# Edge counts by a fixed table, early one-hots, weight sums in K/V, and two jobs back on VectorE, in a fused graph and attention kernel

## The chip, the cores and the metric

The kernel runs on one core of a Trainium2 chip, as one program with one launch. TensorE multiplies matrices into eight PSUM banks; VectorE, ScalarE and GpSimd work on elements; SyncE's queue issues all the DMAs. The metric is the device time of one execution in microseconds (us). Before the change it is 1457.32 us, the median of 3 runs (1456.39 to 1459.52).

## What is computed

The input is `x`, 1250 nodes by 1024 features, a list of 20,000 edges (`src`, `dst`), and weights. One layer is computed:

```
xn = layernorm(x)
x  = x + gnn(xn) + mix(xn)
x  = x + ffn(layernorm(x))

mix: q = relu(xn Wq + bq); k = relu(xn Wk + bk); v = xn Wv + bv
     attn = q (k^T v) / (L * 64), 16 heads; attn Wo + bo
gnn: sage(h, Ws, Wn, b) = h Ws + (A h / deg) Wn + b
     h = relu(sage(xn, Ws0, Wn0, b0)); sage(h, Ws1, Wn1, b1)
ffn: both weights are rounded to -1, 0, 1 times mean(|w|), activations to 127 steps per row
     gelu(xq w1) w2
```

`A` is the matrix of edge counts, 1250 by 1250: entry (d, s) is how many edges go from s to d. The edges are sorted by `dst`.

## The kernel before

Rows of x are worked through in ten tiles of 128. Matrices that need more than half precision are held as a high and a low half in 16 bits, and a product of two such is three passes of matmuls: `product` (line 1384) runs over eight steps kc of 128 rows, each six matmuls of 128x512, 48 in all. The high half is a ScalarE copy, the low half is the value minus the high half, on VectorE.

The stages in order, with TensorE's line for each:

- *K/V*: for each tile k, then v; `kv_sum` (line 1435) adds the tile's k^T v into PSUM. TensorE's order for a tile t is k of t, `kv_sum` of t - 1, the transposes of x for t + 1, v of t. `kv_sum` of t needs the low half of v of t. Beside it, ScalarE adds up squares and absolute values of the weights in chunks of 128x1024 that pass through a ring of four slots, `STREAM`: each tile from 1 to 8 takes six chunks for norms and two for means (line 588), 64 in all, and all of them stand on ScalarE ahead of the high half of v (`v_hi`, line 535). A chunk's load is issued by SyncE when the sum four chunks before it has ended. In tiles 4 to 7 ScalarE also takes the high halves of two chunks of Wq there.
- *Q and M*: q for eight column tiles m (line 1502), and M = (k^T v) Wo for the heads (line 1510). ScalarE takes six chunks of absolute values with each m (line 610), 48 in all.
- *U*: U = q M for ten tiles (line 1398), with `x` and the biases added on the way out: GpSimd adds the biases to x (line 450), VectorE adds that to the product (line 1122), and the sum goes to a scratch in DRAM. U is in units of four banks, and beside it the edge counts are made.
- *z0*: xn Wn0 for ten tiles, with the rest of the counts. After it come the sums over edges, h, z1, and the feed-forward part, which the change does not touch.

The *edge counts* come from one-hots. VectorE compares a constant ramp with each edge's key (`count_dve`, lines 1110 and 1112), two one-hots per chunk of 128 edges, four chunks to a group, in a ring of four groups that lies in `STREAM`. TensorE multiplies the two (`count_pe`, line 1568), four matmuls a group, into one of four banks. The edges fall into 40 ranges of `dst`, and so into parts 1 to 40, with a part 0 that takes the first chunks of the first range. ScalarE copies each finished range out (line 655). Before the change, tile 0 of U has part 0 ahead of its last step, every later tile of U and z0 has two parts, ahead of steps 3 and 6, and the last tile of z0 has parts 37 to 40. The first one-hots can be made only when all 112 weight sums have ended (`stream_used`), because they overwrite `STREAM`; VectorE makes them after the last low half of M.

The weights Wn0 (in U) and Ws0 (in z0) are also split: SyncE loads a chunk into `SPLIT`, ScalarE makes the high half and a scaled copy (lines 516 and 503), and GpSimd subtracts (line 454). Ws0 lies where M was, so its loads are issued after U.

Every engine runs its own program in the order in which it is written; semaphores join them. No planner decides anything.

## Time and profile before

| what | value |
|---|---|
| runs | 1456.39, 1457.32, 1459.52 us |
| profiled execution | 1456.9 us, span 1454.8 us |
| TensorE busy | 1397.5 us, 96% of the span |
| VectorE, ScalarE, GpSimd busy | 738.8, 483.8, 72.9 us |
| chain that ended last | TensorE 70%, VectorE 14%, issue 5%, DMA 5%, ScalarE 4% |
| mean granted clock of TensorE | 0.991 |

The span is the time between the first and the last instruction of the core. Busy time is summed per engine. In the rows below PE is TensorE, PEld its weight loads, DVE VectorE, ACT ScalarE, POOL GpSimd and SPq SyncE's queue; L588 is line 588 of the kernel before. A bracket at a row's end is the time that the engine was idle before it, and the work whose end released it. The granted clock is a share of full speed.

### The profile page before, as it was taken

Reading aid. Unit: us, or ns where it says so; the run is one execution under the profiler, and the core shown is the slowest. Engines: PE = TensorE matmul, PEld = TensorE weight load, DVE = VectorE, ACT = ScalarE, POOL = GpSimd, SP = SyncE. Lnnn points to the kernel's source line nnn. Section 1 sums busy time; section 2 is a strip of 40 time slices with the busy share of each in tenths; the row PEclk is TensorE's granted clock in tenths of the full one; section 3 lists DMA queues with packets and bytes.
Section 4 is the critical chain, followed back from the end, with each engine's and each line's share of the span. In section 5 each row is a group of like instructions: output and inputs, shape, how many; then the busy total and the mean of one; then the engine's idle time right before and its main releaser. Section 6 shows DMA issues by size and latency. Waiting matters only on the chain.

```text
span 1454.8 us, 22724 instructions
## 1 busy us (share of the span) xinstructions
PE 1397.5 (96%) x7442; PEld 677.5 (47%) x7443; DVE 738.8 (51%) x1292; ACT 483.8 (33%) x664; POOL 72.9 (5%) x55
## 2 busy tenths in 40 slices
PE   4999999999699999999999999999999999999998
PEld 2454445555245444444444444444444444444444
DVE  6735452353598645527667422147888453333332
ACT  7646574266412123211221222100000244443342
POOL 0000000000223311100000000000000000000000
PEclk9999999999899999999999999999999999999999
DMA  8356762786323231024455112154564211000100
GB/s 318 104 215 215 263 222 111 261 285 217 143 88 131 101 102 45 15 73 129 146 159 161 41 46 71 72 205 131 185 202 144 100 74 59 30 29 29 58 29 29
DMA packets 55523, 183.13 MB, mean 126 GB/s; under 512 B 6176, under 2 KB 14880, under 8 KB 55200
## 3 DMA queue, kind: packets, MB, share of 16 engines
q1 hardware_dynamic: 55456, 182.26, 36.4%
q8 instruction: 40, 0.66, 0.2%
q14 instruction: 27, 0.22, 0.1%
HBM read 158.11 MB, written 24.12 MB: 125 GB/s over the span
## 4 chain that ended last, share of the span: by engine, by line
PE 70%; DVE 14%; issue 5%; DMA 5%; ACT 4%; DVEq 1%; SPq 1%; ACTq 0%
PE ps L1398 34%; PE ps L1749 10%; PE ps L1735 9%; PE ps L1502 7%; PE ps L1634 4%; DMA SPLIT<-in_Wneigh 3%; DVE XIN L1204 2%; PE ps L1568 2%; DVE SPLIT L1204 2%; PE ps L1405 2%; DVE XIN L1198 1%; DVE SPLIT L1198 1%; DMA STREAM<-in_w1t 1%; PE ps L1435 1%; ACT S L503 1%
## 5 line engine op out<-in xcount | busy, mean ns | idle before, releaser
L1398 PE MATMUL ps<-S,XH 128*128 128x512 f16 x2400 | 529.4, 380 | 1.3 <-ACT XH L710 0.8
L1398 PEld LDWEIGHTS ps<-S,XH 128*128 (+1 forms) x2400 | 232.3, 98 | 274.0 <-issue 1.1
L1634 PE MATMUL ps<-Zb,AT 128*128 128x512 f16 x800 | 177.3, 382 | 7.4 <-DVE TMP L1220 7.4
L1749 PE MATMUL ps<-S,XH 128*128 128x512 fp8e4 x640 | 143.0, 379 | 1.1 <-ACT XH L776 1.1
L1735 PE MATMUL ps<-S,SPLIT 128*128 128x512 fp8e4 x640 | 141.2, 379 | 0.0
L1634 PEld LDWEIGHTS ps<-Zb,AT 128*128 (+1 forms) x800 | 78.0, 98 | 104.7 <-issue 13.0
L1110 DVE TENSOR_SCALAR STREAM<-iota_m,key_m 128x320 f16 x240 | 107.4, 447 | 24.6 <-issue 18.1
L1398 PE MATMUL ps<-Zb,XH 128*128 128x512 f16 x480 | 107.7, 384 | 4.6 <-ACT Zb L503 2.3
L1398 PE MATMUL ps<-S,Zb 128*128 128x512 f16 x480 | 107.3, 380 | 0.0
L1502 PE MATMUL ps<-XH,S 128*128 128x512 f16 (+1 forms) x576 | 102.6, 339 | 0.0
L1735 PEld LDWEIGHTS ps<-S,SPLIT 128*128 128x128 f16 x640 | 62.2, 98 | 73.2
L1749 PEld LDWEIGHTS ps<-S,XH 128*128 128x128 f16 x640 | 61.3, 98 | 69.8 <-issue 1.4
L764 ACT ACTIVATE Zb<-ps,cols 128x512 f32<-128x512 f32 x80 | 54.5, 686 | 118.1 <-PE ps L1735 118.0
L1324 DVE TENSOR_REDUCE AM<-Zb 128x1 f32<-128x1024 f32 x40 | 48.2, 1216 | 58.8 <-ACT Zb L764 58.8
L1502 PEld LDWEIGHTS ps<-XH,S 128*128 128x128 f16 x576 | 56.1, 98 | 47.0 <-issue 2.3
L1398 PEld LDWEIGHTS ps<-Zb,XH 128*128 128x128 f16 x480 | 47.3, 99 | 62.0 <-issue 4.4
L588 ACT ACTIVATE STREAM<-STREAM 128x1024 f32<-128x1024 f32 x64 | 66.9, 1045 | 17.9 <-DMA STREAM<-in_w1t 15.7
L655 ACT ACTIVATE AT<-ps 128x320 f32 (+1 forms) x40 | 17.4, 436 | 165.6 <-PE ps L1573 165.6
L1398 PEld LDWEIGHTS ps<-S,Zb 128*128 (+1 forms) x480 | 45.7, 98 | 53.6 <-issue 1.1
L1112 DVE TENSOR_SCALAR STREAM<-iota_s,key_s 128x128 f16 x240 | 65.4, 273 | 0.0
L1568 PE MATMUL ps<-STREAM 128*128 x240 | 43.3, 310 | 16.8 <-DVE STREAM L1112 16.6
L610 ACT ACTIVATE STREAM<-STREAM 128x1024 f32<-128x1024 f32 x48 | 50.3, 1050 | 17.0 <-DMA STREAM<-in_w2t 11.0
(202 smaller groups left out, 1168.1 us busy)
## 6 DMA issues: line engine op xcount, KB each, us to landing
STREAM<-in_w1t SPq DMA_DIRECT2D x64, 512.0 KB, 4.7
STREAM<-in_w2t SPq DMA_DIRECT2D x64, 512.0 KB, 4.7
STREAM<-in_w_all SPq DMA_DIRECT2D x48, 512.0 KB, 5.7
XIN<-in_x SPq DMA_DIRECT2D x20, 512.0 KB, 5.3
SPLIT<-in_Wneigh SPq DMA_DIRECT2D x16, 512.0 KB, 5.7
SPLIT<-in_Wself SPq DMA_DIRECT2D x16, 512.0 KB, 3.5
u_scratch<-HL SPq DMA_DIRECT2D x10, 512.0 KB, 3.0
XIN<-u_scratch SPq DMA_DIRECT2D x10, 512.0 KB, 6.2
```

The costliest lines, as they stand in the source:

```text
L588: A(STREAM[:, n % 4, :], STREAM[:, n % 4, :], ACT.Square if n < NORMS else ACT.Abs, accum_out=total).then_inc(S("stream_used"), 1)
L610: A(STREAM[:, slot, :], STREAM[:, slot, :], ACT.Abs, accum_out=MW_all[:, bass.ds(c, 1)]).then_inc(S("stream_used"), 1)
L764: A(hid[:, slot, n * BANK:(n + 1) * BANK], banks(n % 4, 1), ACT.Gelu, scale=at("dq1", t)).then_inc(S("gelu"), 1)
L1110: V.tensor_scalar(hot_m[:, bass.ds(r * QUAD + j, 1), :], iota_m[:, :], key_m[:, bass.ds(c_ + j, 1)], None, ALU.is_equal)
L1112: one = V.tensor_scalar(hot_s[:, bass.ds(r * QUAD + j, 1), :], iota_s[:, :], key_s[:, bass.ds(c_ + j, 1)], -float(g * P), ALU.subtract, AL ...
L1204: V.scalar_tensor_tensor(q8[:, n % 2, :], STREAM[:, n, :], col("nthr")[:, w:w + 1], above, ALU.is_lt, ALU.subtract, saturate=False).then_i ...
L1398: last = mm(acc[:, n * BANK:(n + 1) * BANK], left(l, kc), right(kc, r)[:, n * BANK:(n + 1) * BANK], start=(kc == 0 and i == 0), stop=(kc = ...
L1502: last = mm(ps[:, 3 * j * BANK + a:3 * j * BANK + b], Wq_s[:, kc, l, mc], XH[:, r, kc, a:b], start=(kc == 0 and l == 0 and r == 0), stop=( ...
L1568: one = mm(ps[:, at_:at_ + GW], hot_s[:, bass.ds(r * QUAD + q, 1), :], hot_m[:, bass.ds(r * QUAD + q, 1), :], start=False, stop=False, ski ...
L1634: last = mm(banks(bank + n, 1), AT_tile(t, s), Z[:, r, s, n * BANK:(n + 1) * BANK], start=(s == 0 and r == 0), stop=(s == NT - 1 and r == 1))
L1735: last = mm(banks(n % 4, 1), x2_tile[:, j, kc, :], w1q[:, kc, n * BANK:(n + 1) * BANK], start=(kc == 0), stop=(kc == KC - 1))
L1749: last = mm(banks(4 + h, 1), hid_T[:, j, kc, :], w2q[:, kc, h * BANK:(h + 1) * BANK], start=(kc == 0), stop=(kc == HC - 1))
```

## The change

- *Sums.* In K/V each tile takes four chunks of absolute values instead of two, four more come after tile 8, and Q takes four with each of m = 0 to 6, none with m = 7. It remains 112 in all.
- *Early one-hots.* VectorE makes part 0, now three groups instead of four, between q's tiles 6 and 7.
- *Counts by table.* `PARTS` gives the number of parts for each tile of U and z0: one in the first four, two in the next ten, three in the next five, two in the last. One part stands ahead of step 6 (7 in the first tile), two ahead of 3 and 6, three ahead of 2, 4 and 6.
- *VectorE.* GpSimd's additions and subtractions go. VectorE subtracts from the scaled chunk in one operation, and adds the biases to the result of U in a second operation behind the first. In a tile it makes the one-hots of the first part, then the work of the tile before (the result of U or the low half of z0, then the split), then the other one-hots. In U, chunk t of Wn0 is split in tile t + 2; in z0, chunk t of Ws0 in tile t.
- *x and Wn0* are loaded two chunks ahead; the loads of x for U come ahead of the weight chunks of Q.
- The loops over U and z0 are written out.

```diff
-NORMS, KV_MEANS = 6, 2
-Q_MEANS = 6
-Q_FIRST = 8 * KV_MEANS
+NORMS, KV_MEANS = 6, 4
+KV_ALL = NORMS + KV_MEANS
+Q_MEANS = 4
+Q_FIRST = 8 * KV_MEANS + 4
 RING = 4
-FIRST_PART = RING * QUAD
+FIRST_PART = 3 * QUAD
 NB = NG + 1
 LO_UNIT = 256
+PARTS = [1] * 4 + [2] * 10 + [3] * 5 + [2]
+        def parts_of(tile):
+            return range(sum(PARTS[:tile]), sum(PARTS[:tile + 1]))
-                for n in range(NORMS + KV_MEANS):
-                    slot = n % 4
+                for n in range(KV_ALL):
+                    slot = (2 * j + n) % 4
                     if first and n < 4:
                         sp.wait_ge(S("split_lo"), KC + n + 1)
-                    wait(sp, "stream_used", (NORMS + KV_MEANS) * (t - 1) + n - 3)
+                    wait(sp, "stream_used", KV_ALL * (t - 1) + n - 3)
                     chunk = rows(w_all, NORMS * (t - 1) + n) if n < NORMS else \
                         rows(w_flat[0], KV_MEANS * (t - 1) + n - NORMS)
                     sp.dma_start(STREAM[:, slot, :], chunk).then_inc(S(f"stream_in{slot}"), 16)
...
+            def mean_load(w, c, slot):
+                sp.wait_ge(S("stream_used"), c + (8 * NORMS - 3))
+                sp.dma_start(STREAM[:, slot, :], rows(w_flat[w], c - HC * w)).then_inc(S(f"stream_in{slot}"), 16)
+            for n in range(4):
+                mean_load(1, 8 * KV_MEANS + n, n)
...
-            mean_loads(0, Q_FIRST, HC)
-            mean_loads(1, HC, 2 * HC)
             sp.wait_ge(S("ln_xn"), NT)
             load_x(0, 0)
             load_x(1, 1)
-            load_split(Wneigh0, 0, 0, 24)
+            mean_loads(1, Q_FIRST, 2 * HC)
+            for t in range(2):
+                load_split(Wneigh0, t, t, 24 + t)
             def u_moves(t, j, split=True, x_too=True):
                 if split:
-                    load_split(Wneigh0, t + 1, 1 - j, 24 + 1 + t)
+                    load_split(Wneigh0, t, j, 24 + t)
...
-            steps(sp, 0, 6, u_moves)
-            u_moves(6, 0)
-            u_moves(7, 1, False)
+            steps(sp, 0, 2, lambda t, j: u_moves(t, j, split=False))
+            steps(sp, 2, 8, u_moves)
...
-            def u_pool(t, j):
-                pool.wait_ge(S(f"x_in{j}"), 80 + 8 * (t - j) + 16)
-                nc.gpsimd.tensor_tensor(XIN[:, j, :], XIN[:, j, :], b_out, ALU.add).then_inc(S("xb"), 1)
-            def split_pool(dst, kc, slot, idx):
-                pool.wait_ge(S("split_hi"), idx + 1)
-                nc.gpsimd.tensor_tensor(dst[:, kc, 1, :], SPLIT[:, slot, :], dst[:, kc, 0, :],
-                                        ALU.subtract).then_inc(S("split_lo"), 1)
-            def u_split_pool(t, j):
-                u_pool(t, j)
-                split_pool(weight(S0), t, j, 24 + t)
-            pool.wait_ge(S("b_out"), 1)
-            pool.wait_ge(S("split_lo"), 24)
-            steps(pool, 0, 8, u_split_pool)
-            for t in range(8, NT):
-                u_pool(t, t % 2)
-            steps(pool, 0, 8, lambda t, j: split_pool(weight(S1), t, j, 32 + t))
...
-            def split_scaled(dst, kc, slot, idx, scale):
-                act.wait_ge(S(f"split_in{slot}"), 8 * (idx - KC * WQ - slot) + 16)
-                alone(act)
-                A(dst[:, kc, 0, :], SPLIT[:, slot, :], ACT.Copy, scale=scale)
-                split(SPLIT[:, slot, :], SPLIT[:, slot, :], scale)
...
-                    for n in range(NORMS + KV_MEANS):
+                    for n in range(KV_ALL):
...
-                        act.wait_ge(S(f"stream_in{n % 4}"), 32 * (t - 1) + 16 * (n // 4) + 16)
+                        b = 1 - j
+                        slot = (2 * b + n) % 4
+                        act.wait_ge(S(f"stream_in{slot}"), 40 * (t - (1 + b)) + 16 * ((10 * b + n) // 4) + 16)
                         alone(act)
...
+            norm("norm5", 5, 4)
+            for n in range(4):
+                add_up(8 * KV_MEANS + n, n, 20 * 16 + 16)
+            kv_act(9, 1, ln=False, norms=False)
...
+            def q_means(m):
                 for n in range(Q_MEANS):
-                    at_ = Q_MEANS * j + n
-                    add_up(Q_FIRST + Q_MEANS * m + n, at_ % 4, 16 * 16 + 24 * (m - j) + 16 * (at_ // 4) + 16)
+                    add_up(Q_FIRST + Q_MEANS * m + n, n, 21 * 16 + 16 * m + 16)
...
-            q_means(7, 1)
...
+            def counts_act(tile):
+                for part in parts_of(tile):
...
+            for t in range(NT):
+                if t > 1:
+                    split_chunk(weight(S0), t - 2, t % 2, 24 + t - 2, at("s", WN0))
+                counts_act(t)
...
+            for t in range(NT):
+                if t > 0:
+                    z_act("z0", t - 1, 4 * ((t - 1) % 2), Z0_SCALE)
+                if t < KC:
+                    split_chunk(weight(S1), t, t % 2, 32 + t, at("s", WS0))
+                counts_act(NT + t)
...
-            steps(dve, 4, 8, qm_dve)
-            for p in range(5, KC):
-                m_dve(p, M_BANK[p])
-            dve.wait_ge(S("b_out_in"), 32)
-            V.tensor_tensor(b_out, b1_in, b_out, ALU.add).then_inc(S("b_out"), 1)
...
-            def u_out_dve(t, j, first=False):
-                dve.wait_ge(S("u_ps"), t + 1)
-                dve.wait_ge(S("xb"), t + 1)
...
+            steps(dve, 4, 6, qm_dve)
+            qm_dve(6, 0)
             dve.wait_ge(S("bounds"), 1)
             dve.wait_ge(S("iotas"), 3)
             dve.wait_ge(S("stream_used"), 112)
             count_dve(0)
+            qm_dve(7, 1)
+            for p in range(5, KC):
+                m_dve(p, M_BANK[p])
+            dve.wait_ge(S("b_out_in"), 32)
+            V.tensor_tensor(b_out, b1_in, b_out, ALU.add).then_inc(S("b_out"), 1)
+            def u_out_dve(t, j, first=False):
+                dve.wait_ge(S("u_ps"), t + 1)
+                dve.wait_ge(S(f"x_in{j}"), 80 + 8 * (t - j) + 16)
+                if not first:
+                    dve.wait_ge(S(f"u_out{j}"), 8 * (t - j))
+                V.scalar_tensor_tensor(u_out[:, j, :], banks(4 * j), c, XIN[:, j, :],
+                                       ALU.mult, ALU.add).then_inc(S("u_t"), 1)
+                dve.wait_ge(S("u_t"), t + 1)
+                V.tensor_tensor(u_out[:, j, :], u_out[:, j, :], b_out, ALU.add).then_inc(S("u"), 1)
+            def counts_dve(tile, between):
+                parts = list(parts_of(tile))
+                count_dve(parts[0])
+                between()
+                for part in parts[1:]:
+                    count_dve(part)
...
+            def u_dve(t):
+                u_out_dve(t - 1, (t - 1) % 2, t < 3)
+                if t > 1:
+                    split_chunk(weight(S0), t - 2, t % 2, 24 + t - 2, at("s", WN0))
+            dve.wait_ge(S("b_out"), 1)
             for t in range(1, NT):
-                u_dve(t)
+                counts_dve(t, lambda: u_dve(t))
...
             def z0_dve(t):
-                count_dve(2 * t + 19)
                 if t > 0:
                     z_dve("z0", t - 1, 4 * ((t - 1) % 2), Z0_SCALE)
                 else:
                     u_out_dve(9, 1)
-                count_dve(2 * t + 20)
-            z0_dve(0)
-            z0_dve(1)
+                if t < KC:
+                    split_chunk(weight(S1), t, t % 2, 32 + t, at("s", WS0))
+            for t in range(2):
+                counts_dve(NT + t, lambda: z0_dve(t))
...
-            for t in range(2, 9):
-                z0_dve(t)
-            count_dve(37)
-            z_dve("z0", 8, 0, Z0_SCALE)
-            for part in range(38, NB):
-                count_dve(part)
+            for t in range(2, NT):
+                counts_dve(NT + t, lambda: z0_dve(t))
             z_dve("z0", 9, 4, Z0_SCALE)
-            dve.wait_ge(S("split_lo"), 40)
...
-            def counts_between(first_part, j):
-                return {3: lambda: count_pe(first_part, count_bank(2 - 2 * j)),
-                        6: lambda: count_pe(first_part + 1, count_bank(3 - 2 * j))}
-            def u_pe(pair, j, ready=None, between=None):
-                t = pair * 2 + j
+            def counts_between(tile, more={}):
+                parts = list(parts_of(tile))
+                places = {1: (7 if tile == 0 else 6,), 2: (3, 6), 3: (2, 4, 6)}[len(parts)]
...
+            def u_pe(t):
                 wait(pe, "u", t - 1)
-                product(banks(4 * j), lambda l, p: qT[:, l, p, tile_of(t)], of(M_s), ready, "m",
-                        between or counts_between(t * 2 - 1, j)).then_inc(S("u_ps"), 1)
+                product(banks(4 * (t % 2)), lambda l, p: qT[:, l, p, tile_of(t)], of(M_s), 0 if t == 0 else None, "m",
+                        counts_between(t, {7: lambda: pe.wait_ge(S("m_lo"), 8)} if t == 0 else {}))\
+                    .then_inc(S("u_ps"), 1)
...
+            for t in range(NT):
+                u_pe(t)
...
+            def z0_pe(t, more={}):
+                wait(pe, "z0_lo", t - 1)
+                product(banks(4 * (t % 2)), of_x(t), of(weight(S0)),
+                        between=counts_between(NT + t, more)).then_inc(S("z0_ps"), 1)
...
-            z0_pe(4, 1, {3: lambda: count_pe(37, count_bank(0)), 5: lambda: count_pe(38, count_bank(1)),
-                         6: lambda: count_pe(39, count_bank(2)), 7: lambda: count_pe(40, count_bank(3))})
+            for t in range(2, NT):
+                z0_pe(t)
```

On ScalarE, at the last K/V tiles: the sums (written to `NPW` or `MW`) stand ahead of the second copy to `AT`, the high half of v. Before:

```order
L495 ACTIVATE XH<-ps 128x8x128
L531 ACTIVATE AT<-TMP 128x1024
L588 ACTIVATE STREAM,NPW<-STREAM 128x1024 x6
L588 ACTIVATE STREAM,MW<-STREAM 128x1024 x2
L535 ACTIVATE AT<-TMP 128x1024
L500 ACTIVATE cols<-ps 128x5
L531 ACTIVATE AT<-TMP 128x1024
L535 ACTIVATE AT<-TMP 128x1024
```

and now:

```order
L481 ACTIVATE XH<-ps 128x8x128
L510 ACTIVATE AT<-TMP 128x1024
L569 ACTIVATE STREAM,NPW<-STREAM 128x1024 x6
L569 ACTIVATE STREAM,MW<-STREAM 128x1024 x4
L514 ACTIVATE AT<-TMP 128x1024
L486 ACTIVATE cols<-ps 128x5
L582 ACTIVATE STREAM,MW<-STREAM 128x1024 x4
L510 ACTIVATE AT<-TMP 128x1024
L514 ACTIVATE AT<-TMP 128x1024
```

Two more sums stand ahead of the high half, and four between the norms' square root and the high half of k of tile 9.

On VectorE, at the end of Q: `Zb<-AT,Zb` is q's low half, `S<-ps,cols,S` M's low half, and the load of `bnd` begins a part of one-hots. Before:

```order
L1072 SCALAR_TENSOR_TENSOR S<-ps,cols,S 128x1024
L221 REGISTER_ALU
L221 COMPARE_AND_BRANCH
L1072 SCALAR_TENSOR_TENSOR S<-ps,cols,S 128x1024 [waits m_hi] x3
L1087 TENSOR_TENSOR TMP<-AT,TMP 128x1024 [waits b_out_in]
L1100 TENSOR_LOAD bnd [waits stream_used,iotas,bounds]
```

and now:

```order
L954 TENSOR_SCALAR AT<-ps,cols 128x1250 [waits q_lo,q_ps]
L957 SCALAR_TENSOR_TENSOR Zb<-AT,Zb 128x1250 [waits q_hi]
L1034 SCALAR_TENSOR_TENSOR S<-ps,cols,S 128x1024 [waits m_hi]
L1054 TENSOR_LOAD bnd [waits stream_used,iotas,bounds]
...
L1066 TENSOR_SCALAR STREAM<-iota_s,key_s 128x128
L1069 ISA
L1057 COMPARE_AND_BRANCH
L954 TENSOR_SCALAR AT<-ps,cols 128x1250 [waits q_lo,q_ps]
L957 SCALAR_TENSOR_TENSOR Zb<-AT,Zb 128x1250 [waits q_hi]
L1034 SCALAR_TENSOR_TENSOR S<-ps,cols,S 128x1024 [waits m_hi] x4
L1081 TENSOR_TENSOR TMP<-AT,TMP 128x1024 [waits b_out_in]
```

The part that waits for `stream_used` has moved ahead of q's last tile, M's low halves and the addition of the biases.

On VectorE, in the first tile of z0: the result of U's last tile and what follows it. Before:

```order
L1112 TENSOR_SCALAR STREAM<-iota_s,key_s 128x128
L1115 ISA
L1103 COMPARE_AND_BRANCH
L1122 SCALAR_TENSOR_TENSOR HL<-ps,cols,XIN 128x1024 [waits u_out1,xb,u_ps]
L1100 TENSOR_LOAD bnd
```

and now:

```order
L1066 TENSOR_SCALAR STREAM<-iota_s,key_s 128x128
L1069 ISA
L1057 COMPARE_AND_BRANCH
L1088 SCALAR_TENSOR_TENSOR HL<-ps,cols,XIN 128x1024 [waits u_out1,x_in1,u_ps]
L1091 TENSOR_TENSOR HL<-HL,TMP 128x1024 [waits u_t]
L825 SCALAR_TENSOR_TENSOR S<-SPLIT,cols,S 128x1024 [waits split_hi]
L1054 TENSOR_LOAD bnd
```

Between U's last result and the next one-hots there are now the addition of the biases and the split of the first chunk of Ws0, which waits for ScalarE's high half.

## Rows read from the trace of the kernel before

**Rows 1.** Busy time by stretch: engines' us, granted clock, DMA share and rate.

```profile
60.00:257.00 197.00, 194.40 (x1145) 98.00 (x1145) 85.38 (x108) 112.50 (x178) 0.00 (x0) 1.00 0.56 198
384.80:404.20 19.40, 5.14 (x19) 1.83 (x18) 16.32 (x42) 4.79 (x6) 8.79 (x4) 0.58 0.19 75
434.10:446.74 12.64, 12.64 (x69) 6.35 (x68) 10.60 (x34) 2.88 (x5) 4.51 (x2) 1.00 0.37 126
634.00:637.00 3.00, 3.00 (x11) 1.19 (x11) 1.95 (x10) 0.44 (x1) 0.00 (x0) 0.50 0.00 0
```

**Rows 2.** Timeline of ScalarE, tile 4: start, us, line, idle before in brackets.

```profile
143.28 1.04 ACT L588 ACTIVATE STREAM<-STREAM 128x1024 f32<-128x1024 f32 x1
...
148.64 1.06 ACT L588 ACTIVATE STREAM<-STREAM 128x1024 f32<-128x1024 f32 x1 [2.61 <-DMA STREAM<-in_w1t]
...
149.70 1.04 ACT L535 ACTIVATE AT<-TMP 128x1024 f16<-128x1024 f32 x1
```

**Rows 3.** DMA issues, 142.3 to 144.8 us: count, KB, us to landing.

```profile
STREAM<-in_w1t SPq DMA_DIRECT2D x1, 512.0 KB, 5.9
XIN<-in_x SPq DMA_DIRECT2D x1, 512.0 KB, 6.6
SPLIT<-in_Wq SPq DMA_DIRECT2D x2, 512.0 KB, 7.6
```

**Rows 4.** Timeline of SyncE's queue, the same place.

```profile
142.52 0.33 SPq L277 DMA_DIRECT2D STREAM<-in_w1t  x1
143.05 0.33 SPq L239 DMA_DIRECT2D XIN<-in_x  x1
```

**Rows 5.** Timeline of TensorE: K-times-V sums of tiles 1, 4, 7.

```profile
81.97 1.50 PE L1435 MATMUL ps<-AT 128*128 128x128 f16 x24
...
152.14 1.50 PE L1435 MATMUL ps<-AT 128*128 128x128 f16 x24 [1.01 <-DVE AT L907]
...
222.91 1.50 PE L1435 MATMUL ps<-AT 128*128 128x128 f16 x24
```

**Rows 6.** Timeline of ScalarE: V high halves of tiles 1, 7.

```profile
78.17 1.04 ACT L535 ACTIVATE AT<-TMP 128x1024 f16<-128x1024 f32 x1
...
219.89 1.04 ACT L535 ACTIVATE AT<-TMP 128x1024 f16<-128x1024 f32 x1
```

**Rows 7.** Timeline of TensorE: the first edge counts.

```profile
388.84 1.28 PE L1568 MATMUL ps<-STREAM 128*128 x4 [4.02 <-DVE STREAM L1112]
...
401.23 1.26 PE L1568 MATMUL ps<-STREAM 128*128 x4 [8.91 <-DVE STREAM L1112]
```

**Rows 8.** Timelines of GpSimd and VectorE in TensorE's long wait.

```profile
391.90 2.33 POOL L450 TENSOR_TENSOR XIN<-XIN,TMP 128x1024 f32<-128x1024 f32 x1 [91.40 <-ACT SPLIT L503]
...
391.88 2.41 DVE L1112 TENSOR_SCALAR STREAM<-iota_s,key_s 128x128 f16 x1
```

**Rows 9.** Timeline of TensorE, last tile of z0.

```profile
633.28 1.22 PE L1568 MATMUL ps<-STREAM 128*128 x4 [2.37 <-DVE STREAM L1112]
```

**Rows 10.** Timelines of ScalarE and TensorE, first tile of z0.

```profile
528.47 1.15 ACT L516 ACTIVATE S<-SPLIT,cols 128x1024 f16<-128x1024 f32 x1 [10.71 <-DMA SPLIT<-in_Wself]
...
528.01 0.70 PE L1568 MATMUL ps<-STREAM 128*128 x4
```

**Rows 11.** Timelines of ScalarE and VectorE: weight sums, one-hots.

```profile
360.58 1.04 ACT L610 ACTIVATE STREAM<-STREAM 128x1024 f32<-128x1024 f32 x1
...
385.14 0.19 ACT L610 ACTIVATION_READ_ACCUMULATOR STREAM<-STREAM 128x1 f32 x1
...
367.94 1.58 DVE L992 TENSOR_SCALAR AT<-ps,cols 128x1250 f32<-128x1250 f32 x1 [8.47 <-PE ps L1502]
...
378.23 1.22 DVE L1087 TENSOR_TENSOR TMP<-AT,TMP 128x1024 f32<-128x1024 f32 x1
...
386.86 0.30 DVE L1110 TENSOR_SCALAR STREAM<-iota_m,key_m 128x320 f16 x1 [7.42 <-issue]
...
389.08 0.30 DVE L1110 TENSOR_SCALAR STREAM<-iota_m,key_m 128x320 f16 x1 [0.52 <-issue]
```

More of the change, by code:

```diff
@@ L597, in _, with add_up @@
             kv_act(8, 0, ln=False)
+            def add_up(c, slot, count):
+                act.wait_ge(S(f"stream_in{slot}"), count)
+                alone(act)
+                A(STREAM[:, slot, :], STREAM[:, slot, :], ACT.Abs,
+                  accum_out=MW_all[:, bass.ds(c, 1)]).then_inc(S("stream_used"), 1)
             norm("norm5", 5, 4)
+            for n in range(4):
+                add_up(8 * KV_MEANS + n, n, 20 * 16 + 16)
             kv_act(9, 1, ln=False, norms=False)
@@ L695, in _ @@
             act.wait_ge(S("u_ps"), NT)
-            z0_act(0, 0, z=False)
-            z0_act(0, 1)
-            pairs(act, 2, 8, z0_act)
-            z0_act(4, 0, False)
-            count_act(9, 0)
-            z_act("z0", 8, 0, Z0_SCALE)
-            for q in range(1, 4):
-                count_act(9, q)
+            for t in range(NT):
[4 more added lines that the diff above has]
+                counts_act(NT + t)
             z_act("z0", 9, 4, Z0_SCALE)
```

101 lines of the change are left out of this document (27 added, 74 removed).

## The prediction

> **What bounds the kernel now.** I read the page first: TensorE is busy for 96% of the span and the chain that ended last is mostly its matmuls, so only two things can move the time: TensorE's idle stretches, and the stretches in which its clock is granted at half. Then the busy time by stretch: K/V (60 to 257 us) is nearly full, with 2.6 us idle in 197, and its DMA share is 0.56; the stretch from 384.8 to 404.2 us is the large hole, with 5.1 us busy of 19.4 and a mean clock of 0.58 [rows 1]. Then the timelines of single engines around each hole, to see what ends it.
>
> Three places matter.
>
> *K/V, tiles 4 to 6.* ScalarE takes the V high half only after its last weight sum. In tile 4 that sum waits 2.61 us for its load and starts at 148.64, the high half starts at 149.70 [rows 2], and TensorE, which had waited 1.01 us, starts the K-times-V sum at 152.14 [rows 5]: 2.44 us from high half to sum, through VectorE's low half. So here ScalarE and the load queue, not TensorE, set the pace.
>
> *The first edge counts.* TensorE waits 4.02 us for the first one-hots and 8.91 us for the third group [rows 7]. The first wait is ScalarE's: its last weight sum is read at 385.14, and VectorE's first one-hot follows at 386.86 [rows 11]. The second is GpSimd's: while its addition takes 2.33 us, a VectorE one-hot issued beside it takes 2.41 us [rows 8]; four such GpSimd operations stand one behind the other there.
>
> *The last tile of z0.* Four parts of counts stand in it, TensorE waits 2.37 us, its four matmuls take 1.22 us where others take 0.70 [rows 9, 10], and the granted clock is 0.50 afterwards, the lower of the two levels, 1.2 against 2.4 GHz [rows 1].
>
> **The change part by part.** The sum is made against the profiled execution (1456.9 us, span 1454.8); the median of the runs shown is 1457.3, 0.4 above it.
>
> *The hole before U's end of tile 0: a gain of 17.2.* Idle is 19.40 - 5.14 = 14.3 us [rows 1]. The sixteen count matmuls in it take the 5.1 us, at full clock four groups of about 0.55 (a row of 0.70 holds some 0.15 of the last one's end) [rows 10], so 2.9 more is lost to the clock. In the new kernel twelve of the sixteen chunks are made before q's last tile, no GpSimd operation is left in the stretch, and the fourth group and the next three are needed only at step 6 of tile 1, some 9 us later, against 2.2 us a group on VectorE (386.86 to 389.08) [rows 11]. I expect no wait. TensorE's first wait could come back only if VectorE reached the early one-hots late, which is the next term.
>
> *The early one-hots: a loss of 1.3.* They wait for 112 weight sums. The last of these is now the fourth of q's tile 6, which ends at 360.58 + 1.04 = 361.6. From the last sum to the first one-hot is 386.86 - 385.33 = 1.5 us, so 363.1; two groups at 2.22 and a last one of some 1.7 end at 369.2. Behind them on VectorE stands q's tile 7, which began at 367.94 [rows 11], and ScalarE, M's last products and U wait for it. Bounds 0 and 2.2 (one group more).
>
> *Counts by table: a gain of 4.3.* The last tile of z0 has two parts instead of four: 2.4 of waiting, 0.5 on the count matmuls and some 1.4 of the 3 us at half clock behind it go [rows 1, 9]. Bounds 2.4 and 5. Tiles 4 to 8 of z0 take three parts of one group each: 3 x 2.2 and two operations of 1.2 on VectorE, 9 us, less than a tile of U has below, so I put it at nothing, at worst 0.5 a tile.
>
> *Additions and splits on VectorE.* Ten additions and sixteen splits of about 1.22 us each [rows 11] replace GpSimd operations of 2.3 that had stopped VectorE as long [rows 8]. A tile of U with four groups takes TensorE 12.64 us, and VectorE is busy for 10.6 of them, two stops of 2.3 included [rows 1]. Without the stops it is busy 10.6 - 2 x 2.0 + 2 x 1.22 = 9.0. Laid end to end with the loop's own overhead it is 3 x 1.25 + 4 x 2.22 = 12.6, just the tile. The one-hots can be prepared while the long operations run, so I put it at nothing; the other end is a rival.
>
> *The first split of z0: a loss of 7.8.* Before, VectorE made the last bias result of U and went straight to the one-hots. Now the split of W_self0 stands between them, and its load can only be issued after U's last result is stored. ScalarE gets that weight at 528.47, and TensorE took the count of the place at 528.01 [rows 10]. New: the bias addition makes U's last result 1.3 later, so ScalarE starts at 529.8, its half is read at 530.9, VectorE's split ends at 532.1, and 1.98 later (386.86 to 388.84) [rows 7, 11] TensorE can start: 534.1, a wait of 6.1. After waits of this length the clock was at half [rows 1]; I add 1.7, a little more than behind the 2.37 us one. Bounds 4 and 10. Queued behind the waiting split on VectorE are all later one-hots; behind TensorE's wait, everything.
>
> *Weight sums in K/V: a loss of 15.8.* Each tile gets two more sums and two more loads, ahead of the V high half. In tile 4 load 7 was issued at 142.52 and landed 5.9 later, at 148.4; the x load issued at 143.05 landed 6.6 later, at 149.7, and the weight loads behind it took 7.6 in the mean, each some 1.3 after the one before [rows 3, 4]. Loads 8 and 9 can be issued when sums 4 and 5 end, the latter at 143.28 + 1.04 = 144.3 [rows 2], so they take the places of these: the last lands at 151.0, the high half starts at 152.3 instead of 149.7, 2.6 later. In tiles 4 to 6 TensorE waits already, so all of it counts: 7.8. In tile 7 the high half starts at 219.89 and the sum at 222.91, 0.6 of room, so 2.0; in tile 1 it is 78.17 and 81.97, 1.4 of room, so 1.2 [rows 5, 6]. The others have more room. That is 11.0. Bounds: 0, if the loads land as fast as sums end, and 24, if each added load brings the 2.61 us of waiting that load 7 brought [rows 2], 5.2 a tile. TensorE now waits 3.6 us in three tiles and 2.0 in one. Its clock stayed at 1.00 with waits of 1.01 and fell to 0.50 after 2.37 [rows 1, 5, 9]. I add 1.2 for each, 4.8 (bounds 0 and 7).
>
> For one load by itself the Trainium skill gives another price (DMA: Bandwidth & Descriptors, Anatomy of one DMA): about 2.0 us fixed, plus the bytes at 436 GB/s, for a transfer issued by GpSimd. That is an estimate of 3.2 us for 512 KB. The trace does not agree for loads issued close together: 5.9, 6.6 and 7.6 us [rows 3]. By the page load 9 would land at 147.7 and nothing would be lost in K/V; a rival below has that end, from the rows alone.
>
> Q loses twenty weight sums, which changes nothing: TensorE has no wait there. Sum: -17.2 - 4.3 + 1.3 + 7.8 + 15.8 = +3.4. That is 1460.3 for the profiled execution, 1460.7 as a median.
>
> **The rivals.**
>
> *Loads hidden, faster.* With sums of 1.04 us and a deeper queue, loads 8 and 9 land before ScalarE is there, at or before 148.4 to 149.7. Then K/V costs 0 to 3, and the sum is -21.5 + 1.3 + 7.8 + 1.5 = -11: 1446. For it: the DMA share in K/V is only 0.56 [rows 1]. Against: the last sum of tile 4 waits already, and it is the landing that ends its wait. It decides where a shift of 2.6 shrinks below 1.
>
> *Waits without the clock.* All waits come as worked out, but the 3.6 us ones leave the clock alone and the one in z0 costs 4: -21.5 + 1.3 + 4 + 11 = -5: 1452. For it: the waits are spread between full matmul streams. Against: 2.37 us was enough once [rows 9].
>
> *The queue saturates.* Each added load costs 2 us or more instead of 1.3, towards the 2.61 of the bound. Then the shift is 4 to 5.2, K/V loses 17 to 24 plus clock, and the time is 1467 to 1474. Against: behind a full queue the landings are 1.3 apart [rows 3].
>
> *VectorE becomes the bound of U and z0.* If its queue hides none of the overhead, each of the two parts of a tile adds the 0.5 us of idle that stands between groups [rows 11] once more, and the release of the addition 0.2: 13.8 us instead of 12.6, 1.2 in four tiles and 0.5 in five, 7 in all: 1468. It decides where VectorE needs more than the tile's 12.6 us. For it: laid end to end the work is already 12.6. Against: the 9.0 busy.
>
> **How the numbers follow.** Forecast 0.47, loads hidden 0.12, waits without the clock 0.16, the queue saturates 0.14, VectorE the bound 0.11. What a measurement of this kernel can tell from no change is about 0.2%, 2.9 us. The forecast's own spread is about 4 us, so of its 0.47 some 0.25 is slower by more than that, 0.19 the same, 0.03 faster. With the rivals: slower 0.49, same 0.22, faster 0.29. The range goes from 1449 to 1470: it leaves out most of the hidden loads and the far end of the saturated queue. The forecast's own range is 1456 to 1465.
>
> **What would show it.** In the new profile: no wait over 1 us between 376 us and U's tile 2, shifted by what K/V lost; q's tile 7 on VectorE about 1.3 late; K-times-V sums of tiles 4 to 6 each after an idle of 3 to 4 us and periods of 26 to 28 us instead of 24.1; one wait of about 6 us in the first tile of z0, ended by VectorE's one-hots, behind a split that ScalarE released; none in its last tile; the granted clock at half after some of the waits. The forecast is wrong if the K/V tiles keep their 24.1 us, if the wait in z0 is under 3 us, or if TensorE waits for one-hots in the tiles of U.

## The result and the profile after

The changed kernel takes 1470.2 us (median of 4 runs, 1467.28 to 1470.64) against 1458.1 for the kernel before (1456.39 to 1459.52). The ratio is 1.0079 with a 95% interval of 1.0062 to 1.0097, so it is slower by 12 us. The forecast was 1460.7, with a range of 1449 to 1470. The time lies 0.2 above the upper end of that range and outside the forecast's own range of 1456 to 1465.

The stretches that answer to [rows 1], in the changed kernel (columns as there): the K/V stretch, from its second V product to its last K-times-V sum, then the first edge counts, the wait in z0's first tile, and z0's last tile.

```profile
67.30:294.17 226.87, 214.80 (x1220) 110.97 (x1221) 88.50 (x114) 135.96 (x219) 0.95 (x1) 0.97 0.66 237
411.00:428.00 17.00, 16.38 (x85) 7.73 (x84) 10.99 (x43) 1.47 (x2) 0.00 (x0) 1.00 0.18 62
536.00:552.00 16.00, 10.25 (x45) 4.41 (x44) 7.46 (x23) 3.97 (x5) 0.00 (x0) 0.79 0.26 97
640.00:653.00 13.00, 13.00 (x71) 6.37 (x70) 4.49 (x17) 1.90 (x3) 0.00 (x0) 1.00 0.00 0
```

The first of them has 12.1 us of idle time and a mean clock of 0.97; the same stretch of the kernel before had 2.6 us, at 1.00:

```profile
59.90:270.44 210.54, 207.94 (x1221) 105.41 (x1222) 88.50 (x114) 113.65 (x179) 0.95 (x1) 1.00 0.57 205
```

So K/V lost 226.87 - 210.54 = 16.3 us: the idle time grew by 9.5, and the busy time by 6.9, which is the lower clock. The hole at the first counts is gone, and so is the wait in z0's last tile. What held tile 4 stands on ScalarE: the last of the ten sums waits for its load, and the V high half comes behind it:

```profile
159.84 1.06 ACT L569 ACTIVATE STREAM<-STREAM 128x1024 f32<-128x1024 f32 x1 [1.77 <-DMA STREAM<-in_w1t]
...
160.89 1.04 ACT L514 ACTIVATE AT<-TMP 128x1024 f16<-128x1024 f32 x1
```

How such a ledger is made: take one instruction that both kernels have, and subtract its start in the one from its start in the other. Where that difference jumps, time went or came. This is TensorE in the changed kernel, at such places:

```profile
17.79 1.01 PE L1375 MATMUL ps<-ident,HL 128*128 128x128 f16 x8 [17.79 <-ACT HL L476]
...
90.03 1.50 PE L1405 MATMUL ps<-AT 128*128 128x128 f16 x24 [0.50 <-DVE AT L869]
...
163.34 2.01 PE L1405 MATMUL ps<-AT 128*128 128x128 f16 x24 [4.15 <-DVE AT L869]
...
190.82 2.16 PE L1405 MATMUL ps<-AT 128*128 128x128 f16 x24 [2.73 <-DVE AT L869]
...
218.29 2.31 PE L1405 MATMUL ps<-AT 128*128 128x128 f16 x24 [2.73 <-DVE AT L869]
...
245.00 1.77 PE L1405 MATMUL ps<-AT 128*128 128x128 f16 x24 [1.97 <-DVE AT L869]
...
294.17 1.51 PE L1405 MATMUL ps<-AT 98*128 98x128 f16 x24
...
395.34 7.11 PE L1480 MATMUL ps<-S,AT 128*128 128x512 f32 x12 [2.09 <-DVE AT L954]
402.29 9.23 PE L1368 MATMUL ps<-S,Zb 128*128 128x512 f16 x42
...
542.70 1.25 PE L1537 MATMUL ps<-STREAM 128*128 x4 [5.75 <-DVE STREAM L1066]
...
551.60 0.70 PE L1537 MATMUL ps<-STREAM 128*128 x4
...
665.97 2.64 PE L1628 MATMUL ps<-one,AT 128*128 128x2 f16 x100
```

and the ones of before that stand against them (the sums of tiles 1, 4 and 7 are in [rows 5], the count at 528.01 in [rows 10]):

```profile
10.39 1.01 PE L1405 MATMUL ps<-ident,HL 128*128 128x128 f16 x8 [10.39 <-ACT HL L490]
...
270.44 1.50 PE L1435 MATMUL ps<-AT 98*128 98x128 f16 x24
...
375.59 9.23 PE L1398 MATMUL ps<-S,Zb 128*128 128x512 f16 x42
...
535.08 0.70 PE L1568 MATMUL ps<-STREAM 128*128 x4
...
651.37 2.64 PE L1663 MATMUL ps<-one,AT 128*128 128x2 f16 x100
```

| stretch | how much later the changed kernel is at its end, us | change, us | forecast, us |
|---|---|---|---|
| start, to the first transpose | 17.79 - 10.39 = 7.4 | +7.4 | none |
| K/V, to its last sum | 294.17 - 270.44 = 23.7 | +16.3 | +15.8 |
| Q and M, to U | 402.29 - 375.59 = 26.7 | +3.0 | +1.3 |
| U and z0's first counts, without the wait | 542.70 - 5.75 - 528.01 = 8.9 | -17.8 | -17.2 |
| that wait and the clock behind it | 551.60 - 535.08 = 16.5 | +7.6 | +7.8 |
| the rest of z0 | 665.97 - 651.37 = 14.6 | -1.9 | -4.3 |

The spans differ by 14.1 (1468.9 and 1454.8): another 0.5 comes back behind it. The row that no term of the forecast had is the first, and it is most of the error of 9.5 us in the median.

It isn't TensorE's. On GpSimd, in the changed kernel, the first select comes 10.25 us after the fill ahead of it, and nothing that the profile shows holds it ("issue"):

```profile
0.74 0.20 POOL L423 MEMSET ident<- 128x128 f16 x1 [0.29 <-POOLq L1778]
11.20 0.28 POOL L425 TENSOR_SCALAR_AFFINE_SELECT ident<-ident 128x128 f16<-128x128 f16 x1 [10.25 <-issue]
```

In the kernel before, the fill stands at 0.72 and the select at 1.17:

```profile
1.17 0.29 POOL L418 TENSOR_SCALAR_AFFINE_SELECT ident<-ident 128x128 f16<-128x128 f16 x1 [0.24 <-POOL ident L416]
```

VectorE waits for GpSimd's constants before it touches x, so its first instruction starts at 12.20. In the kernel before the constants were ready early, and it started at 4.80, when x had landed. The difference is the 7.4 us of the table. The changed kernel, then the one before:

```profile
12.20 1.29 DVE L796 BATCH_NORM_STATS2 st<-XIN 128x6 f32<-128x512 f32 x2 [12.20 <-POOL cols L436]
...
4.80 1.29 DVE L834 BATCH_NORM_STATS2 st<-XIN 128x6 f32<-128x512 f32 x2 [4.80 <-DMA XIN<-in_x]
```

GpSimd's two programs are alike there, word for word. What the change took from GpSimd are its additions and subtractions of U and z0, 390 us later.

### The profile page after: what moved, and what is told of

Read it like the earlier page. It is cut to its first block, busy times and chain, and to the rows that moved or that the text cites. A ratio compares the mean times of both kernels' runs of the same rounds, so it can differ in the third digit from the quotient of the medians.

```text
span 1468.9 us, 22192 instructions
## 1 busy us (share of the span) xinstructions
PE 1404.6 (96%) x7442; PEld 683.2 (47%) x7442; DVE 731.4 (50%) x1318; ACT 467.0 (32%) x648; POOL 15.4 (1%) x29
## 4 chain that ended last, share of the span: by engine, by line
PE 66%; DVE 15%; issue 6%; DMA 6%; ACT 5%; DVEq 1%; SPq 1%; ACTq 0%; POOL 0%; POOLq 0%
PE ps L1368 31%; PE ps L1714 9%; PE ps L1700 9%; PE ps L1472 6%; PE ps L1599 4%; DMA SPLIT<-in_Wneigh 3%; DVE XIN L1173 2%; PE ps L1537 2%; PE ps L1375 2%; DMA STREAM<-in_w1t 2%; DVE SPLIT L1173 2%; DVE SPLIT L1167 1%; DVE XIN L1167 1%; ACT STREAM L569 1%; PE ps L1405 1%
## 5 line engine op out<-in xcount | busy, mean ns | idle before, releaser
L1368 PEld LDWEIGHTS ps<-S,XH 128*128 128x128 f16 (+1 forms) x2400 | 232.7, 98 | 274.4 <-issue 3.2
L1064 DVE TENSOR_SCALAR STREAM<-iota_m,key_m 128x320 f16 x240 | 72.3, 301 | 42.4 <-issue 27.1
L569 ACT ACTIVATE STREAM<-STREAM 128x1024 f32<-128x1024 f32 x80 | 83.7, 1047 | 20.8 <-DMA STREAM<-in_w1t 18.7
L825 DVE SCALAR_TENSOR_TENSOR S<-SPLIT,cols,S 128x1024 f32 (+1 forms) x40 | 50.8, 1279 | 45.4 <-ACT S L489 45.3
L639 ACT ACTIVATE AT<-ps 128x320 f16<-128x320 f32 x40 | 17.5, 437 | 173.4 <-PE ps L1542 173.4
L1368 PEld LDWEIGHTS ps<-S,Zb 128*128 128x128 f16 x480 | 45.7, 98 | 53.9 <-issue 0.8
L489 ACT ACTIVATE S<-SPLIT,cols 128x1024 f32 (+1 forms) x42 | 47.4, 1139 | 46.4 <-DMA SPLIT<-in_Wneigh 33.3
L1066 DVE TENSOR_SCALAR STREAM<-iota_s,key_s 128x128 f16 x240 | 59.7, 249 | 0.7 <-issue 0.7
```

The costliest lines, as they stand in the source:

```text
L569: A(STREAM[:, slot, :], STREAM[:, slot, :], ACT.Square if n < NORMS else ACT.Abs, accum_out=total).then_inc(S("stream_used"), 1)
L825: V.scalar_tensor_tensor(dst[:, kc, 1, :], SPLIT[:, slot, :], scale, dst[:, kc, 0, :], ALU.mult, ALU.subtract).then_inc(S("split_lo"), 1)
L1064: V.tensor_scalar(hot_m[:, bass.ds(r * QUAD + j, 1), :], iota_m[:, :], key_m[:, bass.ds(c_ + j, 1)], None, ALU.is_equal)
L1066: one = V.tensor_scalar(hot_s[:, bass.ds(r * QUAD + j, 1), :], iota_s[:, :], key_s[:, bass.ds(c_ + j, 1)], -float(g * P), ALU.subtract, AL ...
L1368: last = mm(acc[:, n * BANK:(n + 1) * BANK], left(l, kc), right(kc, r)[:, n * BANK:(n + 1) * BANK], start=(kc == 0 and i == 0), stop=(kc = ...
```

## The experiments

All are timed in three sessions, each beside the kernel before, which had medians of 1458.1, 1459.0 and 1457.5 us. A difference between kernels of different sessions is uncertain by about 1 us. First, four edits of the changed kernel, one for each suspect.

**Two sums a tile in K/V.** The sixteen other sums are left out, with their loads.

```diff
-NORMS, KV_MEANS = 6, 4
+NORMS, KV_MEANS = 6, 2
...
-                    slot = (2 * j + n) % 4
+                    slot = n % 4
```

> The changed kernel with two weight sums and two loads a tile in K/V, as before the change, instead of four. The sixteen other sums are left out (their places get a copy of the first sixteen, one short ScalarE operation); all else stays. Theory (the sums in front of the V high half cost K/V 16.3 us): K/V's tiles 4 to 6 take 24.1 us again with waits of about 1 us, the last K-times-V sum comes 16 us sooner against TensorE's first instruction, and the time is 1470.2 - 16.3 = 1454. Rival (something else in the new K/V part lengthens it, as the added last four sums or the turned slots): the tiles keep over 26 us and the time stays above 1465. On the start, where TensorE's first instruction came 7.4 us later than before behind a GpSimd stall: if that belongs to GpSimd's program, which this edit leaves alone, it is there again.

Measured: 1453.7 us (ratio 0.9972, 0.9961 to 0.9983). The last K-times-V sum comes 277.86 - 19.22 = 258.6 us after the first transpose, against 276.4 in the changed kernel and 260.1 before. TensorE waits for none of the K-times-V sums of tiles 1 to 9, where waits of about 1 us were expected. So the two sums a tile and their loads are all of the K/V term. The stall at the start is there, and longer: 11.68 us.

**The V high half first.** The same ten sums and loads a tile, in another order.

```diff
                         if ln and n == 3:
                             ln_hi(t + 2, j)
+                        if n == KV_ALL - 2:
+                            v_hi(t, j)
...
-                v_hi(t, j)
+                if not norms:
+                    v_hi(t, j)
```

> The changed kernel with the V high half of each K/V tile moved in front of the last two weight sums of that tile. No work is taken away. Theory (what costs is that the high half queues behind two more sums on ScalarE, not the sums or the loads themselves): the waits of tiles 4 to 7 shrink to about those of before (1.0, 1.1, 0.5, 0) and K/V gives back 13 to 16 us: 1454 to 1457. Rival (the load queue sets the pace: ten stream loads, two splits and one x load a tile at about 1.3 us each): the last two sums then hold up the next tile's high halves, the waits come back at another place, and at most 5 us are won: 1465 to 1470.

Measured: 1451.8 us (ratio 0.9963, 0.9949 to 0.9977). That is 2 us below the range expected. K/V takes 257.0 us, 3.1 less than in the kernel before, whose own small waits (2.6 us in all) are gone too. The four stretches of 25 us that have a mean clock of 0.93 in the changed kernel now stand so:

```profile
157.00:182.00 25.00, 25.00 (x157) 12.98 (x156) 11.81 (x14) 18.58 (x31) 0.00 (x0) 1.00 0.84 308
182.00:207.00 25.00, 25.00 (x169) 13.37 (x167) 11.83 (x14) 17.91 (x29) 0.00 (x0) 1.00 0.81 306
207.00:232.00 25.00, 25.00 (x148) 12.54 (x146) 13.21 (x15) 18.05 (x29) 0.00 (x0) 1.00 0.80 282
232.00:257.00 25.00, 25.00 (x136) 12.15 (x135) 5.21 (x5) 17.52 (x32) 0.00 (x0) 1.00 0.62 211
```

The transfers run at up to 308 GB/s with TensorE full; in the same stretches the changed kernel has 227 to 247. So the load queue can bring all ten chunks a tile without holding up TensorE. What cost 16 us is that the one ScalarE operation that TensorE needs stood behind sums whose loads were still on their way. The rival of a slow queue falls, in this kernel's K/V.

**The first split of z0 behind the one-hots.**

```diff
-                if t < KC:
+                if 0 < t < KC:
                     split_chunk(weight(S1), t, t % 2, 32 + t, at("s", WS0))

             for t in range(2):
                 counts_dve(NT + t, lambda: z0_dve(t))
+                if t == 0:
+                    split_chunk(weight(S1), 0, 0, 32, at("s", WS0))
```

> The changed kernel with VectorE's split of the first W_self0 chunk moved behind the second part's one-hots in the first tile of z0. Theory (the 5.75 us wait there is the one-hots queued behind the waiting split, and 1.83 us more are the clock behind it): no wait over 1 us in z0's first tile, no half clock behind it, the time 1470.2 - 7.6 = 1462.6. Rival (the bias addition makes the one-hots late by itself, so a wait of 1 to 3 us and a part of the clock loss remain): 1464 to 1467.

Measured: 1460.8 us (ratio 1.0022, 1.0013 to 1.0032). TensorE goes through the place without a wait:

```profile
528.90 0.70 PE L1539 MATMUL ps<-STREAM 128*128 x4
...
533.38 0.70 PE L1539 MATMUL ps<-STREAM 128*128 x4
```

The gain is 9.4 and not 7.6 between the medians. Between the profiled runs it is 10.2, and 2.5 of that is a shorter K/V part, in which this edit changes nothing (see the spread below).

**A longer GpSimd program.**

```diff
+            for n in range(26):
+                nc.gpsimd.memset(pad[:, n:n + 1], 0.0)
```

> The changed kernel with 26 one-column fills at the very end of GpSimd's program, which makes it as long as before; nothing reads them and nothing waits for them. In the changed kernel GpSimd stood still for 10.25 us behind its first fill, and VectorE and TensorE started 7.4 us late. Theory (the stall comes from how the shorter GpSimd program lies and is fetched): GpSimd goes on at 1.2 us, TensorE's first transpose is at 10.4 us again, the time is 1470.2 - 7.4 = 1462.8. Rival (the stall has nothing to do with that program's length): it is there again, at 10 us, and the time stays within 0.2% of 1470.2.

Measured: 1470.5 us (ratio 1.0083, 1.007 to 1.0097), with the gap at 9.99 us. This first theory of the start fell: 26 more instructions at the program's end leave the gap as it is.

The gap had come in all five kernels without GpSimd's additions, and not in the one with them. Behind the partition reduction the changed kernel's GpSimd does only fills and copies; before, its next instruction but one was an addition. That gave the second theory, tested in two runs.

**One small addition behind the reduction.**

```diff
             nc.gpsimd.memset(qT[:, :, :, N:NP_], 0.0).then_inc(S("pad0"), 1)
+            pool.wait_ge(S("fills"), 2)
+            nc.gpsimd.tensor_tensor(pad[:, :], ones[:, 0:32], ones[:, 32:64], ALU.add)
```

> The changed kernel with one GpSimd addition of 128x32 elements added behind its partition reduction and fill (about 322 us), where nothing waits for GpSimd; its result is read by nobody. In all kernels without GpSimd additions the engine stood still for 10 to 11.7 us at its first select (0.9 to 11.2 us), whatever the program's length. Theory (the reduction leaves GpSimd so that its next select or addition has to wait some 6 to 10 us, memory fills and copies don't; before the change the additions of U took that wait, now the first select of the next execution does): the small addition comes with a gap of 5 to 6 us behind the fill, GpSimd's select is back at 1.2 us, TensorE's first transpose at 10.4, and the time is 1470.2 - 7.4 = 1462.8. Rival (the stall belongs to the start itself): still there, within 0.2% of 1470.2.

Measured: 1464.1 us (ratio 1.0032, 1.0019 to 1.0045), 6.1 below the changed kernel, whose ratio was 1.0079. GpSimd's timeline, the start and the place of the reduction:

```profile
1.43 0.29 POOL L426 TENSOR_SCALAR_AFFINE_SELECT ident<-ident 128x128 f16<-128x128 f16 x1 [0.50 <-POOL ident L424]
...
316.47 0.81 POOL L450 PARTITION_ALL_REDUCE AT<-AT  x1 [37.48 <-DVE AT L994]
317.16 0.58 POOL L453 MEMSET Zb<- 128x480 f16 x1
325.53 0.24 POOL L455 TENSOR_TENSOR pad<-ones 128x32 f32<-128x32 f32 x1 [7.79 <-issue]
```

The gap has moved to where nobody waits: an addition of 0.24 us has 7.79 us ahead of it (5 to 6 were expected), and the start is clean, with the first transpose at 10.00. The time is 1.3 above the 1462.8 expected. The profiled run was the slowest of the six: K/V took 279.2 us in it, 2.8 more than in the changed kernel's.

**The same addition in the kernel before.**

> The kernel before, with the same small GpSimd addition behind its partition reduction. Theory (the first real addition of U at 391.9 us also had that wait in it, since its x tile was there by about 386.5): GpSimd's first addition starts 3 to 5 us sooner, its four long operations end at 397 to 398 instead of 400.7, TensorE's 8.91 us wait shrinks by about 3, and the time is 1458.07 - 3 = 1455. Rival (no such wait): the addition starts at 391.9 and the time stays within 0.1%.

Measured: 1456.6 us (ratio 0.9981, 0.9972 to 0.999), 2.3 less than its own kernel in that session. GpSimd's real additions:

```profile
309.18 0.24 POOL L448 TENSOR_TENSOR pad<-ones 128x32 f32<-128x32 f32 x1 [8.59 <-issue]
386.32 2.34 POOL L453 TENSOR_TENSOR XIN<-XIN,TMP 128x1024 f32<-128x1024 f32 x1 [76.90 <-DMA XIN<-in_x]
...
395.76 2.12 POOL L457 TENSOR_TENSOR S<-SPLIT,S 128x1024 f32 x1
```

The first now starts when its x tile lands, 386.32 instead of 391.90 [rows 8]. So some 5.6 us of this gap stood in the old hole as well, put down there to ScalarE. The hole, from the end of U's first steps to TensorE's next ones, is 16.9 us long (385.21 to 402.06) against 19.3 before, about the 2.3 us won.

**The one-hots behind M.** What closed the hole?

```diff
-            count_dve(0)
             qm_dve(7, 1)
             for p in range(5, KC):
                 m_dve(p, M_BANK[p])
...
+            count_dve(0)
```

> The changed kernel with the first three groups of one-hots made behind M's last low halves and the bias sum, where they stood before the change, instead of ahead of q's last tile. Theory A (the hole before was GpSimd's additions stopping VectorE and the late last weight sum, and both are gone anyway; the early place only costs): the one-hots run from about 380 us in the clock of the kernel before, 9 us ahead of TensorE's need, no wait at the first counts; the waits of 2.09 us ahead of M's last parts go, with the half clock behind them, and the time is 1470.2 - 3 = 1467. Theory B (the early place is what closed the hole): TensorE waits 2 to 8 us at the first counts and the time is 1471 to 1478.

Measured: 1469.8 us (ratio 1.0075, 1.0061 to 1.0088). The time alone says little: it lies between the 1467 of theory A and the 1471 of theory B. The profile says theory A: no wait at the first counts, and from K/V's last sum (298.65) to U (403.72) it takes 105.1 us, as in the kernel before, against 108.1 in the changed kernel.

```profile
395.84 5.71 PE L1480 MATMUL ps<-S,AT 128*128 128x512 f32 x12
401.90 1.98 PE L1480 MATMUL ps<-S,AT 128*128 128x512 f32 x4 [0.35 <-DVE S L1034]
403.72 9.23 PE L1368 MATMUL ps<-S,Zb 128*128 128x512 f16 x42
412.78 0.17 PE L1530 MATMUL ps<-iota_m,zero 128*128 128x2 f16 x1
412.81 2.15 PE L1537 MATMUL ps<-STREAM 128*128 x12
```

The profiled run was the slowest of the five, at 1473.9 us. Against that of the changed kernel it lost 4.3 us in K/V, 280.7 us long, and 2.0 in the stages behind z0. This edit touches neither.

**The sums where they were, one-hots behind M, additions on VectorE.**

```diff
-NORMS, KV_MEANS = 6, 4
+NORMS, KV_MEANS = 6, 2
...
-Q_MEANS = 4
-Q_FIRST = 8 * KV_MEANS + 4
+Q_MEANS = 6
+Q_FIRST = 8 * KV_MEANS
```

> The changed kernel with the weight sums where they were before the change (two a tile in K/V, six a tile in Q, the last ones behind M) and the one-hots behind M; additions and splits stay on VectorE, the table stays. It tells how much of the 17 us hole belonged to GpSimd's additions and how much to the late last sum. Theory (GpSimd's four operations cost the third and fourth wait, the late sum the first): TensorE waits 4.0 us for the first one-hots, then 0.9 and about 0.9, all three groups at half clock, some 8 us in all instead of 17; K/V as in the kernel before, M without the 3 us. Against the kernel with two sums (1453.7) that is -3 + 8: 1458.7. Rival (the late sum is most of it): the hole comes back with 14 us or more, 1465.

Measured: 1460.5 us (ratio 1.0021, 1.0011 to 1.0031), 1.8 above the 1458.7 expected and 4.5 below the rival's 1465. The waits came as worked out, the first 0.5 longer:

```profile
395.31 1.25 PE L1535 MATMUL ps<-STREAM 128*128 x4 [4.55 <-DVE STREAM L1064]
397.49 1.25 PE L1535 MATMUL ps<-STREAM 128*128 x4 [0.93 <-DVE STREAM L1064]
399.67 1.25 PE L1535 MATMUL ps<-STREAM 128*128 x4 [0.94 <-DVE STREAM L1064]
400.72 10.13 PE L1366 MATMUL ps<-S,Zb 128*128 128x512 f16 x42
```

From the end of U's first steps to TensorE's next step it is 400.72 - 390.59 = 10.1 us. Before it was 403.97 - 384.66 = 19.3, with a fourth group of counts (0.55); in the changed kernel it is 2.1. The late last sum was thus worth about 8.0 us of the hole, and GpSimd's operations about 8.6.

**The changed kernel again.**

> The changed kernel as it is, once more, for the spread of its K/V part: in kernels that share its K/V code the part from TensorE's first transpose to the last K-times-V sum took 273.9 to 280.7 us, with the waits of tiles 4 to 7 and the clock behind them changing from run to run. All theories expect 1467 to 1472, GpSimd's stall of about 10 us at the start, and a K/V part between 273 and 281 us.

Measured: 1470.9 us (ratio 1.009, 1.0074 to 1.0106), stall 10.15 us, K/V 275.5 us. Over the six profiled runs of kernels with this K/V code, that part took 273.9, 275.5, 276.0, 276.4, 279.2 and 280.7 us: a spread of 7 that the forecast's one number hid. The stages behind z0, which are the same in all twelve profiled runs, took 801.9 to 806.0 us. Terms of 1 or 2 us are therefore read from the stretch itself and not from the time of the kernel.

**The edits together:** high half first, split behind, one-hots behind M, one small addition.

> The changed kernel with the four edits together: the V high half in front of the last two sums of a K/V tile, the first W_self0 split behind the second part's one-hots, the one-hots behind M, and the small GpSimd addition. If they are independent the gains add: 18.4 (measured) + 7.6 (the wait and its clock in the trace) + 3 + 7.4 = 36, so 1434. If the place of the one-hots matters (theory B above) it is 1438 to 1442; if the start's stall stays, 1441.

Measured: 1435.4 us (1433.88 to 1435.72), ratio 0.9837 with an interval of 0.9824 to 0.9851 against the kernel before, and 35 us below the changed kernel. K/V takes 257.1 us, the rows that held the waits have none:

```profile
9.97 1.01 PE L1383 MATMUL ps<-ident,HL 128*128 128x128 f16 x8 [9.97 <-ACT HL L479]
...
150.53 1.50 PE L1413 MATMUL ps<-AT 128*128 128x128 f16 x24
...
372.12 9.23 PE L1376 MATMUL ps<-S,Zb 128*128 128x512 f16 x42
381.19 0.17 PE L1538 MATMUL ps<-iota_m,zero 128*128 128x2 f16 x1
381.21 2.16 PE L1545 MATMUL ps<-STREAM 128*128 x12
```

The expectation was 1434. That the gains add up fits the profiles: each edit removes a wait that no other edit was covering.

## Why the prediction was right and wrong

The direction was right, and so were the largest terms. The time was 9.5 above the forecast, and none of the rivals was what happened. "The queue saturates" gave 1467 to 1474, which holds the measured time. But it rests on a shift of 4 to 5.2 us a tile, and TensorE's waits in tiles 4 to 7 grew by 3.1, 1.7, 2.2 and 2.0. The range reached up to 1470 for that rival and for VectorE as the bound; that the time came out at its end, through a term that neither had, is luck.

The signs named ahead of the result nearly all came: no wait over 1 us around the old hole, periods of 26.7 to 27.5 us in tiles 4 to 7, one wait of 5.75 us in z0's first tile and none in its last. The start had no sign.

- *The start, no term, +7.4.* This is the step that failed: the sum put the start at nothing without a reason. The forecast costed GpSimd's operations at what they took and what they stopped, and did not ask what else hung on them. One added operation of 0.24 us, some 325 us into the execution, brings the early start back. So the select at 1.17 us was no property of the code at the start; it hung on what GpSimd runs later in the execution. The profile did hold a hint: GpSimd's first addition started at 391.90 with the cause "ScalarE", while its x tile had been issued at 379.8 and, by the 6.6 us of [rows 3], was there at about 386.4. The 5.5 us in between had no explanation, and were not asked after.
- *K/V, forecast 15.8, measured 16.3.* The mechanism stood as worked out. In tile 4 the high half was forecast at 152.3, which is 160.35 in the changed kernel (8.05 later at that point); it came at 160.89. The split between the parts was less good: 9.5 of waiting (forecast 11.0) and 6.9 of clock (4.8). Waits of 4.15, 2.73, 2.73 and 1.97 us each had half-clock matmuls behind them. That 15.8 met 16.3 so closely is luck in part: over the six profiled runs with this K/V code the loss is 13.8 to 20.7. The prediction's picture that "ScalarE and the load queue" set the pace was only half of it: the order on ScalarE is enough, since the same loads cost nothing with the high half ahead of the last two sums.
- *The hole, forecast -17.2, measured -17.8.* Of this, 1.65 are three groups of count matmuls that the table moves into z0, so the hole itself is 16.1, 1.1 less than forecast. The step named two causes, the late sum and GpSimd; the runs give them 8.0 and 8.6. But it credited the early one-hots, and those were not needed: with the last sum in time, one-hots behind M are ready too.
- *The early one-hots, forecast +1.3, measured +3.0.* Mis-sized. q's last tile starts on VectorE at 393.70. Less the 23.7 of K/V and the start that is 370.0, 2.0 late and not 1.3: the groups are 2.46 and 2.41 us apart there, not 2.2, and 1.9 us pass between the last sum and the first one-hot, not 1.5. The rest, about 1, is the clock behind the wait of 2.09: twelve of M's matmuls took 7.1 us, where eight and four had taken 5.7. No clock was forecast here. Of the six other profiled runs with this order the clock stayed up in five, where eight of M's matmuls behind the wait took 3.70 us, as before; in the sixth, the longer GpSimd program, nine took 5.82.
- *z0's first split, forecast +7.8, measured +7.6*, with a wait of 5.75 for 6.1 and 1.8 of clock for 1.7. Removing the cause removed all of it.
- *Counts by table, forecast -4.3.* Measured is -1.9 net. In it are 1.65 of loss for the three groups that moved in, some 0.2 for the short matmuls that open and close the three added parts, and 0.8 for one group in each of four tiles with three parts, which takes 0.74 us and not 0.54. The gain in the last tile is thus about 4.6, as the trace of the kernel before has it: from its count at 627.59 to 651.37 it took 23.8 us, where the same work at full clock and without a wait takes an estimated 19.2 (from the 13.5 us that 60 matmuls and one group take in the changed kernel, 652.45 to 665.97). The size was near; the groups that the table adds to z0 were left out.
- *VectorE as the bound of U and z0, costed at nothing.* It was nothing: two tiles of U with four groups stand 12.64 us apart (457.62 to 470.26), as before [rows 1], and outside z0's first tile the longest idle time at a count is 0.62 us.

Without its first row the table ends at 7.2 instead of 14.6. The forecast's sum was 3.4. The three groups that changed rows cancel, and the difference of 3.8 is made of 0.5 in K/V, 1.7 at the early one-hots, 1.1 in the hole, -0.2 at z0's first split and 0.7 in the rest of z0.

## What to carry to other kernels

Put the one operation that the bound engine waits for ahead of the filler work on its engine, not behind it: the same loads and sums cost 16 us in one order and nothing in the other. When an engine is relieved of all its work of a kind, look at what its remaining instructions then stand next to, across the end of the execution too. And when a start time in the old profile is some microseconds later than its inputs explain, settle why before the instruction is removed.
